# A fused block of mamba, gated recurrence and two expert layers: the product of expert scores and activated dots on GpSimd instead of VectorE

## The reference

```python
x = x + attn_a(layernorm(x))    # mamba: conv, 16 states, scan over 512 tokens; ff and layer norm
x = x + ffn(layernorm(x))       # experts, "e1" in the kernel
x = x + attn_b(layernorm(x))    # gated recurrence with 16 states
x = x + ffn(layernorm(x))       # experts, "e2", the same weights

def ffn(x):                                  # 8 heads, 2 x 32 keys per head, 8192 experts
    q = (x @ w_q).reshape(b, n, 2, HEADS, DIM_KEY)
    sim = einsum('pbnhd,hkpd->pbnhk', q, keys)
    # the best key of each of the two halves gives score and expert index
    scores, index = best of sx + sy, ix * 32 + iy
    h = einsum('bnd,bnhkd->bnhk', x, w_down[index])
    h = gelu(h) * relu(scores)
    return einsum('bnhk,bnhkd->bnd', h, w_up[index])
```

## Time and profile before

| | us |
|---|---|
| three runs | 2188.92, 2182.73, 2184.6 |
| median | 2184.6 |
| span of the profiled execution | 2189.7 |
| busy in the span: PE, PEld | 1681.9 (77%), 937.5 (43%) |
| busy: DVE, ACT, POOL | 1767.2 (81%), 1543.5 (70%), 1355.7 (62%) |
| L1466, 1024 indirect fetches on POOL | 980.8 busy |
| L1272, the 64 products that the change moves | 56.3 busy, mean 0.880 each |

### The profile page before, as it was taken

How to read it: one execution, slowest core, us unless ns; L and a number is a source line. 1 busy time by engine, 2 the same in 40 slices (tenths; PEclk the granted TensorE clock), 3 DMA queues, 4 the chain that set the end, 5 groups by cost and what they waited for, 6 DMA issues and landing times. The chain is left out here.

```text
span 2189.7 us, 24718 instructions
## 1 busy us (share of the span) xinstructions
PE 1681.9 (77%) x6097; PEld 937.5 (43%) x6186; DVE 1767.2 (81%) x4204; ACT 1543.5 (70%) x3276; POOL 1355.7 (62%) x1209
## 2 busy tenths in 40 slices
PE   4887878787887978888888879788878877754562
PEld 2332435354544545454544444454544444433342
DVE  3898989798988989898898989898889997733331
ACT  4565868587877868787878778777877765554542
POOL 0226463667776667677676676677677776566554
PEclk8898989998999999998999989999989988886776
DMA  2001120222222222222222222322222222233222
GB/s 54 0 10 56 32 65 23 62 66 75 82 80 77 70 84 68 82 77 65 84 80 77 73 84 68 84 68 74 76 75 82 72 80 73 71 87 92 78 82 71
DMA packets 79901, 151.06 MB, mean 69 GB/s; under 512 B 20584, under 2 KB 46592, under 8 KB 79680
## 3 DMA queue, kind: packets, MB, share of 16 engines
q0 software_dynamic: 49152, 134.28, 21.3%
q1 hardware_dynamic: 29344, 14.65, 2.4%
q10 hardware_dynamic: 1248, 0.34, 0.1%
HBM read 145.01 MB, written 4.19 MB: 68 GB/s over the span
## 5 line engine op out<-in xcount | busy, mean ns | idle before, releaser
L1466 POOL DMA_INDIRECT rows<-in_experts,index x1024 | 980.8, 958 | 477.6 <-issue 363.2
L1352 DVE TENSOR_TENSOR_SCAN hp<-dA,fed_ps 128x1024 f32<-128x1024 f32 x256 | 582.3, 2275 | 7.0 <-issue 5.8
L783 PE MATMUL ysum<-hp,ident 128*128 128x512 f32 x1024 | 503.9, 637 | 16.0 <-DVE hp L1362 9.0
L1481 POOL TENSOR_TENSOR hp<-hp,c_row 128x1024 f32<-128x1024 f32 x112 | 263.9, 2356 | 279.2 <-ACT c_row L1043 179.8
L1336 DVE TENSOR_TENSOR fed_ps<-du,b_ps 128x1024 f32<-128x1024 f32 x256 | 313.4, 1224 | 58.4 <-remote 26.3
L1026 ACT ACTIVATE dA<-delta,decay 128x511 f32<-128x511 f32 x512 | 334.8, 711 | 15.8 <-issue 7.9
L1005 ACT ACTIVATE rows<-rows,coef 128x128 f32<-128x128 f32 x1024 | 311.0, 390 | 19.2 <-DVE coef L1272 19.2
L783 PEld LDWEIGHTS ysum<-hp,ident 128*128 128x128 f32 x1024 | 215.0, 211 | 251.3 <-issue 218.5
L1265 DVE CUSTOM_DVE_ANT_0 rows<-rows,xn 128x128 f32<-128x128 f32 x1024 | 261.5, 318 | 51.7 <-DMA rows<-in_experts,index 51.2
L933 ACT ACT_TABLE_LOAD x218 | 279.7, 1283 | 8.8 <-PEq L543 5.0
L716 PE MATMUL bank<-rows,ident 128*128 128x256 f32 x1024 | 247.4, 397 | 34.0 <-ACT rows L1005 33.4
(11 more groups left out here) (182 smaller groups left out, 2357.6 us busy)
## 6 DMA issues: line engine op xcount, KB each, us to landing
rows<-in_experts,index POOLq DMA_INDIRECT x1024
x_in<-in_x SPq DMA_DIRECT2D x16, 256.0 KB
x_res<-in_x SPq DMA_DIRECT2D x16, 256.0 KB
y<-x SPq DMA_DIRECT2D x16, 256.0 KB
rows<-in_taps SPq DMA_DIRECT2D x1, 512.0 KB
rows<-in_wq_t SPq DMA_DIRECT2D x1, 512.0 KB, 5.3
rows<-in_in_proj_t ACTq DMA_DIRECT2D x1, 256.0 KB
rows<-in_key_t SPq DMA_DIRECT2D x1, 128.0 KB, 5.2
```

Of the source, the lines that this page charges most:

```text
L783: mm = nc.tensor.matmul(ysum[:, j, :], ident[:], hp[:, BUFFER[k], j, :], start=(k == SUM_ORDER[0]), stop=(k == SUM_ORDER[-1]))
L1352: nc.vector.tensor_tensor_scan(flat, dA[:, n % NDA, :, :].rearrange("p a b -> p (a b)"), fed_ps[:].rearrange("p a b -> p (a b)"), 0.0, ALU ...
L1466: pool.indirect_dma_start(e.rows[:, t, h, :], None, A["experts"], bass.IndirectOffsetOnAxis(ap=e.index[:, t, h:h + 1], axis=0)).then_inc(e ...
L1481: pool.tensor_tensor(state, state, c_row[:, k % NCR, :].unsqueeze(1).to_broadcast([P, NH, T]), ALU.mult).then_inc(pool_read, 1)
```

## The change

`experts_weigh` moves from VectorE's program to GpSimd's. It waits there for `e.indexed` and `e.gelu` and multiplies `score` with `act`; the maximum with 0 is no longer in it. The tables keep the slots and only rename the stage from `dve_weigh` to `pool_weigh`. In GpSimd's slot it stands behind the state multiply and the products of delta and ahead of the fetches of the same slot.

VectorE's `experts_index` now begins with the sum of maxima (`score`), ahead of the wait for the codes, and behind a wait that the product of the batch before is done (`e.weighed`), since `score` is overwritten. Between `code` and `index` stands the clamp of `score` at 0. The semaphore `picks` counts three steps for a half instead of two.

```diff
-    "dve_weigh_e1": (POST, (72, 85)),
+    "pool_weigh_e1": (POST, (72, 85)),
-    "dve_weigh_e2": (POST, (227, 243)),
+    "pool_weigh_e2": (POST, (227, 243)),
...
+                if later(n):
+                    dve.wait_ge(e.weighed, at(n - 1, 2, half))
+                nc.vector.tensor_tensor(e.score[:, tiles, :], e.top[:, tiles, 0:HEADS], e.top[:, tiles, HEADS:GR],
+                                        ALU.add).then_inc(e.picks, 1)
                 dve.wait_ge(e.coded, at(n, 2, half))
                 nc.vector.tensor_scalar(e.bits[:, tiles, :], codes, 23, None,
                                         ALU.logical_shift_right).then_inc(e.picks, 1)
-                nc.vector.tensor_tensor(e.score[:, tiles, :], e.top[:, tiles, 0:HEADS], e.top[:, tiles, HEADS:GR],
-                                        ALU.add)
-                dve.wait_ge(e.picks, at(n, 4, 2 * half))
+                dve.wait_ge(e.picks, at(n, 6, 3 * half + 1))
...
-                dve.wait_ge(e.picks, at(n, 4, 2 * half + 1))
+                nc.vector.tensor_scalar(e.score[:, tiles, :], e.score[:, tiles, :], 0.0, None, ALU.max)
+                dve.wait_ge(e.picks, at(n, 6, 3 * half + 2))
...
-            def experts_weigh(e, n, half):
-                tiles = slice(half * HALF, (half + 1) * HALF)
-                dve.wait_ge(e.gelu, at(n, 2, half))
-                nc.vector.scalar_tensor_tensor(out=e.coef[:, tiles, :], in0=e.score[:, tiles, :], scalar=0.0,
-                                               in1=e.act[:, tiles, :], op0=ALU.max,
-                                               op1=ALU.mult).then_inc(e.weighed, 1)
...
+            def experts_weigh(e, n, half):
+                tiles = slice(half * HALF, (half + 1) * HALF)
+                pool.wait_ge(e.indexed, at(n, 2, half))
+                pool.wait_ge(e.gelu, at(n, 2, half))
+                pool.tensor_tensor(e.coef[:, tiles, :], e.score[:, tiles, :], e.act[:, tiles, :],
+                                   ALU.mult).then_inc(e.weighed, 1)
...
+                    for m, r, k in due("pool_weigh_e1", i, q, slot):
+                        experts_weigh(e1, m, k)
+                    for m, r, k in due("pool_weigh_e2", i, q, slot):
+                        experts_weigh(e2, m, k)
                     for m, r, k in due("pool_fetch_e2", i, q, slot):
```

More of the change, by code:

```diff
@@ L199 @@
     "dve_dot_e1": (POST, (55, 59, 66, 72)),
-    "dve_weigh_e1": (POST, (69, 73)),
+    "pool_weigh_e1": (POST, (69, 73)),
     "dve_stats_b": (POST, (99,)),
@@ L209 @@
     "dve_dot_e2": (POST, (220, 230, 230, 242)),
-    "dve_weigh_e2": (POST, (232, 244)),
+    "pool_weigh_e2": (POST, (232, 244)),
     "pool_x1": (POST, (3,)),
@@ L1419, in iteration @@
                         nc.vector.tensor_tensor(m20[:], m20[:], rs0[:], ALU.mult).then_inc(p_square, 1)
-                    for m, r, k in due("dve_weigh_e1", i, q, slot):
-                        experts_weigh(e1, m, k)
                     for m, r, _ in due("dve_stats_b", i, q, slot):
@@ L1436, in iteration @@
                                                      0.0, ALU.mult, ALU.add).then_inc(b_scanned, 1)
-                    for m, r, k in due("dve_weigh_e2", i, q, slot):
-                        experts_weigh(e2, m, k)
                 if isinstance(i, int) and i == -1:
```

## The result

The changed kernel takes 2246.35 us (median of 4 runs, 2242.92 to 2254.26), the kernel before 2185.59 us beside it (4 runs, 2182.73 to 2188.92). The ratio is 1.0287, 95% interval 1.0264 to 1.0311: the change costs 60.8 us. The forecast was +38.5. The side and the range were right, the size was 22 us short, and, as the runs show, for a reason that stands in none of its terms.

A forecast was written before the change was run, and what follows sets the result against it. No engine was taken as full: time is lost in handovers, so what counts is where that of coef ends last. -10.9 + 23.5 + 25.9 = +38.5 on 2184.6 gave 2223 us, range 2185 to 2250.

The forecast's parts named there:

- The multiplication leaves VectorE: VectorE: dots behind e1's product take its stall, the scan behind e2's runs free; index chains 0, bounds -6 and +6.
- What is late next is ScalarE: Behind ten held e2 first-half products, only ScalarE's idle time ahead of its next flip copy can be recovered: -10.9 us.
- Price on GpSimd: Each product on GpSimd takes 0.25 us (bounds 0.2 and 1.27), 0.4 with handover; GpSimd's idle time mostly hides it.
- Its place in the loop, +23.5: e2's second-half product stands behind eight e1 fetches: 53.3 us late over eleven batches, 29.8 covered by idle time, +23.5 us.
- The drain, +25.9: After the loop, e2's products stand behind all 32 fetches of their batch: 2.7 + 8.5 + 7.3 + 7.4 = +25.9 us.
- three large terms: Drain: e2's first halves of batches 13, 14 and 15 scaled late, behind the last fetch: +8.5, +7.3 and +7.4 us.
- Batch 12's +2.7: Drain, second half of batch 12: GpSimd must wait for gelu before its next fetch, +2.7 us.
- E: Loop lateness isn't shared with ScalarE's idle time, waits for TensorE's transposes come on top: +68, 2253 us; chance 0.10.
- B: Loop lateness disappears in ScalarE's waits and slack later in the iteration: -10.9 + 25.9 = +15, 2200 us; chance 0.15.
- C: All of VectorE's held time comes back, loop lateness falls into waits: -45.5 + 25.9 = -19.6, 2165 us; chance 0.08.
- D: The wait only changes its owner on VectorE, lateness in loop and drain is covered: 2185 us, within 0.3%; chance 0.09.
- the two late places: GpSimd's product behind queued fetches: e2's second half in the loop (+23.5 us), e2's products in the drain (+25.9 us).

The follow-up runs named there:

- run 1: Kernel before with VectorE's edits alone (maxima added ahead of the wait, sum clamped, plain product still on VectorE): 2185.87 us, ratio 1.0027.
- run 6: As run 4, but e2's first-half product is back on VectorE, in loop and drain: 2194.54 us, ratio 1.0064.
- run 4: Changed kernel with both product slots earlier: e2's second half in the loop (243 to 238), first half in the drain (232 to 223): 2214.63 us, ratio 1.0163.
- run 10: Changed kernel with the loop's second portion of the e1 fetch in slot 45 instead of 43: 2260.32 us, ratio 1.0355.
- run 9: Kernel before with only the second portion of the e1 fetch moved from slot 43 to 45: 2199.74 us, ratio 1.0079.
- run 2: Changed kernel with the loop's slot of e2's second-half product 238 instead of 243: 2226.36 us, ratio 1.0200.
- run 3: Changed kernel with the drain's slot of e2's first-half product 223 instead of 232, ahead of the last 8 fetches: 2213.36 us, ratio 1.0154.
- 7: Changed kernel with only e2's first-half product of the loop on GpSimd, all others on VectorE at their old slots: 2185.05 us, ratio 1.0016.
- run 8: As 7, with the loop's second portion of the e1 fetch in slot 45 instead of 43: 2168.95 us, ratio 0.9952.
- 5: As run 4, with the loop's second portion of the e1 fetch in slot 45 instead of 43: 2192.43 us, ratio 1.0053.
- 12: As run 1, with the second portion of the e1 fetch in slot 45 instead of 43: 2201.73 us, ratio 1.0088.

## Why the prediction was right in sign and short in size

- **The multiplication leaves VectorE: right.** The dots behind e1's product take its stall (1.90 us at 1101.08), the scan behind e2's runs free, and state 9 is 2.5 us earlier. The index chains came to +6 (run 1), the upper bound that was given.
- **"What is late next is ScalarE ... Only that idle time can be recovered; over the ten it sums to -10.9": this step failed,** in size and in sign. VectorE kept its 2.5 us through state 9, and lost 4.3 at state 12. I looked for what is late next on ScalarE alone and not at GpSimd, whose wait for the index, the 2.51 us at 1124.95, I had counted among the 37 us of idle time that hide work. It was that wait which broke the row of fetches. Taking the product back (run 6 against run 4) gains 20 us where the forecast would have lost 11. In the range all the same, the forecast owes part of that to luck, as the sum below shows.
- **Price on GpSimd: right.** 0.236 us median (0.214 to 0.314) against 0.25, and ScalarE waits 0.40 us between gelu and scaling at 2226.54, below, as counted. The Trainium skill's factor of about two ("GPSIMD Engine Reference", section "4.1 Engine selection") is 0.236 / 0.173 = 1.4 here, with VectorE's plain product of run 1; it has the right direction.
- **Its place in the loop, +23.5: over-sized as it stands in this kernel.** "ScalarE, every loop iteration, scaling of e2's second half with about 5 us of idle time" was not seen: in the loop ScalarE waits seven times for `coef`, 23.3 us in all, where 53.3 us of lateness in eleven batches had been counted. The lateness of the product is real, but ScalarE had been made late by the lag (iteration 9, above). With the lag away the lateness shows: the step to state 14 is 5.6 us longer in run 10, where the split alone makes it 2.4 longer (run 9). What moving the product ahead is worth in the loop as it stands isn't shown: 12 us in the trace of run 2, none on top of the drain slot.
- **The drain, +25.9: right** in its three large terms, measured 27.2 in all. ScalarE ahead of the first halves of batches 13, 14 and 15 and at the end, and GpSimd's last fetch and product, against the earlier trace rows:

```profile
2090.73 4.78 ACT L1005 ACTIVATE rows<-rows,coef 128x128 f32<-128x128 f32 x16 [8.01 <-POOL coef L1466]
...
2153.97 4.78 ACT L1005 ACTIVATE rows<-rows,coef 128x128 f32<-128x128 f32 x16 [10.48 <-POOL coef L1466]
...
2215.28 4.78 ACT L1005 ACTIVATE rows<-rows,coef 128x128 f32<-128x128 f32 x16 [21.10 <-POOL coef L1466]
2225.65 0.38 ACT L998 ACTIVATE x<-bank 128x256 f32<-128x256 f32 x1 [5.59 <-PE bank L716]
2225.93 0.21 ACT L993 ACTIVATE act<-dot 128x16 f32<-128x16 f32 x1
2226.54 4.78 ACT L1005 ACTIVATE rows<-rows,coef 128x128 f32<-128x128 f32 x16 [0.40 <-POOL coef L1466]
```

```profile
2214.04 0.95 POOL L1458 DMA_INDIRECT rows<-in_experts,index  x1 [0.30 <-issue]
2215.01 0.23 POOL L1466 TENSOR_TENSOR coef<-score,act 128x16 f32<-128x16 f32 x1
```

  Batch 15 is as drawn: the scaling starts right behind the last fetch, and gelu of the second half (2225.93) right behind x out. The waits grew from 1.80 to 8.01, 1.57 to 10.48 and 12.16 to 21.10, that is by 6.2, 8.9 and 8.9, 24.0 in all, where 23.2 were forecast. Batch 12's +2.7 did not come as drawn: GpSimd didn't wait for gelu there, its product at 2016.68 stood straight behind a fetch, and ScalarE waited 1.12 us for it. In the same place of run 3 the wait of batch 15 is 8.73:

```profile
2178.87 4.78 ACT L1005 ACTIVATE rows<-rows,coef 128x128 f32<-128x128 f32 x16 [8.73 <-POOL coef L1466]
```

- **The rivals.** E's 2253 lies nearest by time, but not by its mechanism: ScalarE's waits did cover the lateness. B, C and D fall with the +60.8. Of C's idea, that all of VectorE's held time comes back, runs 7 and 8 leave this: the time of e2's held first-half product can be kept, if the fetches are rearranged with it.

As a sum, undoing the change from one end (each ratio against its own before, 1% being 21.8 us): 2.87% changed, 1.63% without the two late places, 0.64% with the e2 first-half product back as well, 0.27% with only VectorE's edits left. So the places are worth 27 us (forecast 49), the first-half product 22 (forecast -11), and the rest 8 + 6 = 14 (forecast 0). 27 + 22 + 14 = 63 for the 60.8 measured. By the intervals of the ratios each term is good to some 5 to 8 us. Three misses, -22, +33 and +14, partly cancelled; that the time fell inside the range was luck to that extent. The steps are not additive, as run 10 shows, and other orders of undoing would split them in another way. The 8 us between runs 6 and 1 (e1's products and e2's second half on GpSimd) are hardly clear of noise and were not taken apart.

## To carry to other kernels

A wait on an engine that is off the critical path can be part of the balance: when a faster step removes it, ask what that engine will now do without a pause, and who works beside it. When a small instruction moves to the engine that issues the transfers, place it by what is queued ahead of it there, once for the loop and once for the drain, and expect that two latenesses of one consumer hide each other, so that mending one of them alone shows the other.

## What was not expected of the hardware

While GpSimd issues a row of eight to twelve indirect fetches, what TensorE has finished is reported late, and in a bunch. In the changed kernel the report of the sum over e2's first half came 2.9 to 3.4 us after the start of the row's last fetch in ten of eleven iterations (5.6 in the other), whether the sum's record ended 0.5 or 2.1 us before that start. In the kernel before, where the eight stand behind a pause of 2.4 us or more in all iterations but one, it came anywhere from 0.2 us ahead of that start to 2.7 behind it. With the row broken ahead of the sum the lag is 0.01 us in five kernels out of five (5, 8, 9, 10 and 12). It is so at full granted clock too (1.00 from 1142 to 1156 in run 10), and while GpSimd multiplies: in iteration 7 of run 8 the report comes at 886.39, 0.01 us behind the record, and the state multiply runs from 884.39 to 886.75. So neither the clock nor that multiply makes the lag. Halving the bytes leaves it at 3.9 us, so it goes with the fetches in a row rather than with what they move. Why it is TensorE's reports, and whether the work or only its report is late (the ends of matmuls are modelled in these records, and some records are missing), stays open: no run here separates them.
